# Head sums of two tiles streamed as one: GpSimd scales and adds the squares of two tiles that share a layout of eight heads

## The reference, cut to what matters

```python
x = x + conv(group_norm(x), ...)         # x: 32 images, 384 channels, 1024 pixels; 32 groups

w   = einsum('bnc,oc->bno', xt, qkv_w)   # heads: 12 of d = 32 channels
s   = sum_d((w / ||w||_over_n) ** 2)     # per head and pixel
Pi  = softmax(s * temp, over the 12 heads)
Pi_n = Pi / (sum_n Pi + 1e-8)
dots = einsum('bhn,bhnd->bhd', Pi_n, w * w)
out  = -(w * Pi) / (1 + dots)
y    = einsum('bnc,oc->bno', out, out_w) + out_b
```

## Time and profile before

| | |
|---|---|
| median of 3 runs | 867.25 us (867.11 to 867.55) |
| span of the profiled execution | 864.9 us, first to last instruction |
| PE busy | 851.6 us (98%) |
| DVE busy | 750.2 us (87%) |
| ACT busy | 528.3 us (61%) |
| POOL busy | 232.6 us (27%) |

### The profile page before, as it was taken

The page is one execution under the profiler, slowest core; times in us unless marked ns, Lnnn a source line. Parts: engine busy times, 40 slices in busy tenths (PEclk is TensorE's granted clock), DMA queues, the critical chain, the costliest instruction groups (busy, mean ns, idle before and its releaser), DMA issues.

```text
span 864.9 us, 14022 instructions
## 1 busy us (share of the span) xinstructions
PE 851.6 (98%) x4290; PEld 677.7 (78%) x4290; DVE 750.2 (87%) x1396; ACT 528.3 (61%) x680; POOL 232.6 (27%) x106
## 2 busy tenths in 40 slices
PE   7999999999999999999999999999999999999997
PEld 6767788777787777787777787777887777887776
DVE  7989889898888888888888898888898888898777
ACT  3567656567555677556676556676565675566642
POOL 2432123332123331133331233321233321233300
PEclk9999999999999999999999999999999999999999
DMA  7324665544664544664535654445655446645225
GB/s 279 119 79 153 225 229 185 185 148 169 225 227 161 197 146 181 226 223 160 180 150 198 228 213 168 163 145 220 227 186 196 141 163 225 228 175 186 88 86 197
DMA packets 45259, 157.42 MB, mean 182 GB/s; under 512 B 19866, under 2 KB 23962, under 8 KB 37274
## 3 DMA queue, kind: packets, MB, share of 16 engines
q1 hardware_dynamic: 36856, 154.10, 48.5%
q10 hardware_dynamic: 8354, 2.85, 1.3%
HBM read 104.47 MB, written 52.45 MB: 181 GB/s over the span
## 4 chain that ended last, share of the span: by engine, by line
PE 92%; DVE 4%; issue 1%; DMA 1%; ACT 1%; DVEq 0%; ACTq 0%
PE acc L678 86%; PE spread_ps L800 5%; DVE stats L906 1%; DVE WS L1041 1%; DMA PIB<-pi 0%; DMA X<-in_x 0%; DVE WV L1101 0%; DVE X L1149 0%; PE acc L655 0%; DVE WS L1080 0%; ACT WS L501 0%; DMA pi<-PIT 0%; DVE X L1116 0%; ACT WV L512 0%; PE spread_ps L815 0%
## 5 line engine op out<-in xcount | busy, mean ns | idle before, releaser
L424 POOL TENSOR_TENSOR XL<-XN,XH 128x1024 fp32r<-128x1024 f32 x93 | 222.9, 2414 | 571.7 <-ACT XH L529 548.2
L501 ACT ACTIVATE WS<-acc 128x1024 f32<-128x1024 f32 x96 | 98.4, 1026 | 240.5 <-PE acc L678 197.1
L678 PE MATMUL acc<-XH,W1H 128*128 128x512 f32 x574 | 177.3, 390 | 0.1
L678 PE MATMUL acc<-XH,W1L 128*128 128x512 f32 x574 | 176.8, 389 | 0.0
L678 PE MATMUL acc<-UH,W2H 128*128 128x512 f32 x558 | 172.6, 390 | 1.3 <-ACT WV L512 1.2
L678 PE MATMUL acc<-UH,W2L 128*128 128x512 f32 x558 | 172.3, 390 | 0.0
L678 PE MATMUL acc<-XL,W1H 128*128 128x512 f32 x576 | 146.2, 389 | 0.0
L678 PE MATMUL acc<-UL,W2H 128*128 128x512 f32 x558 | 145.3, 396 | 0.0
L1149 DVE SCALAR_TENSOR_TENSOR X<-acc,bias,X 128x1024 f32<-128x1024 f32 x93 | 116.3, 1276 | 31.0 <-PE acc L678 31.0
L678 PEld LDWEIGHTS acc<-UL,W2H 128*128 128x128 f32 x558 | 102.3, 188 | 32.2 <-issue 11.9
L678 PEld LDWEIGHTS acc<-XL,W1H 128*128 128x128 f32 x576 | 108.0, 188 | 22.7 <-POOL XL L434 0.3
(11 more groups left out here) (119 smaller groups left out, 501.3 us busy)
## 6 DMA issues: line engine op xcount, KB each, us to landing
PIB<-pi SPq DMA_DIRECT2D x94, 528.0 KB, 5.1
X<-in_x SPq DMA_DIRECT2D x31, 1536.0 KB, 6.3
out_y<-X SPq DMA_DIRECT2D x30, 1536.0 KB, 6.5
gathered<-stats_rows ACTq DMA_DIRECT2D x28, 72.0 KB, 5.1
pi<-PIT SPq DMA_DIRECT2D x94, 16.5 KB
X<-in_x SPq DMA_DIRECT2D x3, 512.0 KB, 4.7
out_y<-X SPq DMA_DIRECT2D x1, 1024.0 KB, 6.0
out_y<-X SPq DMA_DIRECT2D x2, 512.0 KB, 2.6
```

Source lines behind the costliest of these rows:

```text
L424: pool.tensor_tensor(XL[:, t, :], XN[:, t, :], XH[:, t, :].bitcast(F32), ALU.subtract).then_inc(xl_done, 1)
L501: act.activation(square_tile(i, t), acc[:, t, :], ACT.Square, accum_out=sumsq[:, t:t + 1]).then_inc(squared, 1)
L678: last = pe.matmul(out[:, h * BANK:(h + 1) * BANK], w[:, k, m * P:(m + 1) * P], r[:, k, h * BANK:(h + 1) * BANK], start=(n == 0 and k == 0 ...
```

## The change

Tiles 0 and 1 get one common layout: eight heads of sixteen channels in each tile, where each had four heads of thirty-two. The weights' columns are ordered so in the prologue (GpSimd's copy of the second weights becomes two copies, and TensorE's turns write other columns); tile 2 keeps its four heads. Since a partition then means the same head in tiles 0 and 1, the scaled squares of both can be added before the head sum. For images 2 to 31:

- GpSimd multiplies the squares of tile 0 and of tile 1 by the inverse sums (one scalar a partition) and adds the two (`pair_squares`: two `tensor_scalar`, one `tensor_tensor`, 128x1024 each), ahead of its `x_lo`.
- TensorE's head sums stream the paired tile and tile 2, eight matmuls where there were twelve.
- VectorE makes the inverse sums of tiles 0 and 1 in `pair_weights`, two small instructions between the last `weigh` and the first `u_lo`; `head_sum_weights` is left with tile 2.
- The rows are spread for two bands (eight heads, four heads) in two transfers of 528 KB where there were three; the first waits for two of the three writes. `attention` takes its sums in two reductions where there was one. The first and last image move all three tiles' rows.

```diff
-HEADSUM_STEPS = 3
+HEADSUM_STEPS = 5
+PAIR_STEPS = 4
+PAIRED = 2
+BAND = (0, 0, 1)
...
+        paired = sb("paired", [P, 2, N])
...
+        def paired_sums(j):
+            return j.follows(PAIRED)
...
-                    for t in tiles:
-                        sp.wait_ge(pi_written[t], rows_moved(j, t, 16))
-                        heads = pi_dram[t * HPT:(t + 1) * HPT].unsqueeze(0)\
-                            .to_broadcast([D, HPT, BLOCKS * QUADS * (QUAD + 1)])
-                        sp.dma_start(PIB[:, t].rearrange("p b n -> p (b n)"), heads).then_inc(pi_spread[t], 16)
+                    for band, of_band in enumerate(BAND_HEADS):
+                        for t in range(of_band.start // HPT, of_band.stop // HPT):
+                            sp.wait_ge(pi_written[t], j.counts(16, 16))
+                        heads = pi_dram[of_band.start:of_band.stop].unsqueeze(0)\
+                            .to_broadcast([P // len(of_band), len(of_band), BLOCKS * QUADS * (QUAD + 1)])
+                        sp.dma_start(PIB[:, band].rearrange("p b n -> p (b n)"), heads).then_inc(pi_spread[band], 16)
...
+            def pair_squares(i):
+                if has(i):
+                    pool.wait_ge(headsum_step, i.counts(HEADSUM_STEPS, 2))
+                    pool.wait_ge(squared, i.counts(T, 2))
+                    pool.wait_ge(scores_done, i.counts(1))
+                    pool.sem_inc(pair_step, 1)
+                    for t in range(2):
+                        pool.tensor_scalar(paired[:, t, :], square_tile(i, t), inv[:, 1, t:t + 1], None, ALU.mult)\
+                            .then_inc(pair_step, 1)
+                    pool.wait_ge(pair_step, i.counts(PAIR_STEPS, 3 - PAIR_STEPS * PAIRED))
+                    pool.tensor_tensor(paired[:, 0, :], paired[:, 0, :], paired[:, 1, :], ALU.add).then_inc(pair_step, 1)
             def step(i):
+                if paired_sums(i):
+                    pair_squares(i)
                 for t in range(T):
                     x_lo(i + 1, t)
...
-                for t in range(T):
+                if paired_sums(i):
+                    pe.wait_ge(pair_step, i.counts(PAIR_STEPS, PAIR_STEPS - PAIR_STEPS * PAIRED))
+                    streams = [(head_temp[:, 0, :], paired[:, 0, :]), (headsum[:, T - 1, :], square_tile(i, T - 1))]
+                else:
+                    streams = [(headsum[:, t, :], square_tile(i, t)) for t in range(T)]
+                for n, (weights, squares) in enumerate(streams):
                     for q in range(QUADS):
...
+            def pair_weights(j):
+                link = chain(headsum_step, j.counts(HEADSUM_STEPS))
+                dve.wait_ge(squared, j.counts(T, 2))
+                dve.wait_ge(scores_done, j.counts(1))
+                link(dve.tensor_scalar(inv[:, 0, 0:2], sumsq[:, 0:2], NORM_FLOOR ** 2, None, ALU.max))
+                link(dve.reciprocal(inv[:, 1, 0:2], inv[:, 0, 0:2]), follows=False)
...
-                    done = dve.tensor_reduce(total, PIB[:, :, :, QUAD], AX_X, ALU.add)
+                    dve.tensor_reduce(total[:, 0:2], PIB[:, 0, :, QUAD].unsqueeze(1).to_broadcast([P, 2, BLOCKS * QUADS]),
+                                      AX_X, ALU.add).then_inc(u_step, 1)
+                    done = dve.tensor_reduce(total[:, 2:3], PIB[:, 1, :, QUAD], AX_X, ALU.add)
...
                 weigh(i - 1, 2)
+                pair_weights(i)
                 u_lo(i - 1, 0)
                 u_lo(i - 1, 1)
```

More of the change, by code:

```diff
@@ L90, in conv_attention @@
     HPT = P // D
+    PAIR_HEADS = 2 * HPT
+    PAIR_D = P // PAIR_HEADS
+    BAND_HEADS = (range(0, PAIR_HEADS), range(PAIR_HEADS, HEADS))
     HALVES = N // BANK
@@ L208, in conv_attention @@
         pi_written = [sem(f"pi_written_{t}") for t in range(T)]
-        pi_spread = [sem(f"pi_spread_{t}") for t in range(T)]
+        pi_spread = [sem(f"pi_spread_{band}") for band in range(BANDS)]
         u_step = sem("u_step")
@@ L260, in pe_spread, with band_rows @@
             return 2 if j.follows(1) else 1
-        def rows_moved(j, t, more=0):
-            return j.counts(16, more - (16 if t == 0 and True else 0))
+        def band_rows(t):
+            return PIB[:, BAND[t], :, 0:QUAD]
+        def paired_sums(j):
+            return j.follows(PAIRED)
         def tile_steps(j, t, steps):
@@ L415, in _ @@
             pool.wait_ge(w2_loaded, 16)
-            pool.tensor_copy(mixed_w2.rearrange("p (m d h) -> p m d h", d=D, h=HPT),
-                             raw_w2.rearrange("p (m h d) -> p m d h", d=D, h=HPT)).then_inc(w2_mixed, 1)
+            for band in BAND_HEADS:
+                columns, h = slice(band.start * D, band.stop * D), len(band)
+                pool.tensor_copy(
+                    mixed_w2.rearrange("p (t c) -> p t c", t=T)[:, :, columns].rearrange("p t (d h) -> p t d h", h=h),
+                    raw_w2.rearrange("p (t c) -> p t c", t=T)[:, :, columns].rearrange("p t (h d) -> p t d h", h=h))\
+                    .then_inc(w2_mixed, 1)
             def x_lo(j, t):
@@ L796, in head_sums @@
                     pe.wait_ge(sm_step, i.counts(SM_STEPS))
-                for t in range(T):
+                if paired_sums(i):
[4 more added lines that the diff above has]
+                for n, (weights, squares) in enumerate(streams):
                     for q in range(QUADS):
-                        block_q = square_tile(i, t).rearrange("p (b q r) -> p q b r", q=QUADS, r=QUAD)[:, q]
-                        last = pe.matmul(scores[q * QUAD:(q + 1) * QUAD, 0:N // QUADS], headsum[:, t, :],
-                                         block_q, start=(t == 0), stop=(t == T - 1))
+                        block_q = squares.rearrange("p (b q r) -> p q b r", q=QUADS, r=QUAD)[:, q]
+                        last = pe.matmul(scores[q * QUAD:(q + 1) * QUAD, 0:N // QUADS], weights, block_q,
+                                         start=(n == 0), stop=(n == len(streams) - 1))
                 last.then_inc(scores_done, 1)
@@ L987, in head_sum_weights @@
                     return
-                link = chain(headsum_step, j.counts(HEADSUM_STEPS))
+                tiles = slice(T - 1, T) if paired_sums(j) else slice(0, T)
+                done = HEADSUM_STEPS - 3 if paired_sums(j) else 0
+                link = chain(headsum_step, j.counts(HEADSUM_STEPS, done))
                 dve.wait_ge(squared, j.counts(T, T))
-                link(dve.tensor_scalar(inv[:, 0, :], sumsq[:], NORM_FLOOR ** 2, None, ALU.max))
-                link(dve.reciprocal(inv[:, 1, :], inv[:, 0, :]))
+                link(dve.tensor_scalar(inv[:, 0, tiles], sumsq[:, tiles], NORM_FLOOR ** 2, None, ALU.max))
+                link(dve.reciprocal(inv[:, 1, tiles], inv[:, 0, tiles]))
                 if j.follows(1):
@@ L995, in head_sum_weights @@
                     dve.wait_ge(temp_kept, 3)
-                link(dve.tensor_tensor(headsum[:], head_temp[:],
-                                       inv[:, 1, :].unsqueeze(2).to_broadcast([P, T, QUAD]), ALU.mult), follows=False)
+                weights = headsum[:, tiles, :]
+                dve.tensor_tensor(weights, head_temp[:, tiles, :], inv[:, 1, tiles].unsqueeze(2).to_broadcast(weights.shape),
+                                  ALU.mult).then_inc(headsum_step, HEADSUM_STEPS - 2 - done)
+            def pair_weights(j):
+                if not has(j):
+                    return
+                link = chain(headsum_step, j.counts(HEADSUM_STEPS))
[3 more added lines that the diff above has]
+                link(dve.reciprocal(inv[:, 1, 0:2], inv[:, 0, 0:2]), follows=False)
             def softmax_shift(j):
```

51 lines of the change are left out of this document (27 added, 24 removed).

## The result

The changed kernel takes 1084.99 us (median of 4 runs, 1082.34 to 1091.92), the kernel before 867.4 us beside it (867.11 to 867.93): 1.252 times the time, 95% interval 1.248 to 1.256. The forecast was slower, 931 us with a range of 860 to 970, so its sign was right and its size was not: 218 us lost where 64 were forecast. The profiled execution took 1091.92 us, its span is 1090.1.

The account below looks back on a forecast made before the run. TensorE was taken to bound the kernel, its chain never leaving it. A 2.6 us wait less 0.45 saved gives 2.15 us an image, 64 us over 30 images: 867.25 + 64 = 931 us, range 860 to 970.

Parts of the forecast that it names:

- The bound and the saving: TensorE's order sets the time; one tile fewer in a head sum saves 0.45 us an image, 13.5 us in all.
- The wait: TensorE waits ahead of every head sum for GpSimd's addition: 2.6 us an image.
- 0.2 + 2d: TensorE's wait at each head sum when two u_lo, two scalings and the addition run one after the other.
- d: Time of one GpSimd scaling of 1024 columns, not in the trace: taken as 1.2 us, range 0.93 to 1.99.
- The hold: VectorE's two u_lo and GpSimd's pair work exclude each other, holding GpSimd the full 2.40 us; chance 0.65.
- The sum: Wait of 2.6 less saving of 0.45 gives 2.15 us an image, 64 us over 30 images.
- The late rows: Rival: first spread waits for the second write, some 0.6 us later, so time stays near 867; chance 0.05.
- VectorE's 0.54 us of new work: Extra reduction and pair_weights on VectorE, covered by 1.02 us idle before L990; otherwise 0.54 us an image.
- The two rivals without a hold: GpSimd undisturbed by u_lo: quick scaling gives 854 to 857 us (chance 0.16), slow scaling about 867 to 912 (0.14).
- the faster one: Rival of no hold and scaling below 1.23 us: 10 to 13.5 us gained, 857 to 854; chance 0.16.

Follow-up runs that it names:

- The halves: Changed kernel without GpSimd's scalings and addition, first band's rows read back in two 264 KB transfers, the first behind the first write alone: 856.9 us, 0.988.

## Why the prediction was right in sign and wrong in size

**The bound and the saving: right.** TensorE's order set the time, and two rounds of a head sum are worth 0.40 us a period by the run with one tile left out; 0.45 was forecast.

**The wait: right in place and mechanism, too small.** It stands where it was forecast, ahead of every head sum, released by GpSimd's addition. By the prediction's own form, 0.2 + 2d, it was 2.6 us with d = 1.2. Measured it is 5.28 us (20.13 - 14.85) in most images. The step that failed is d: "I take 1.2", with 2.41 as the upper end because two operands cost that much (the copy's 1.99 in the range). A scaling of one operand takes 2.84 us, above the two-operand instruction. With it the form gives 0.2 + 5.68 = 5.88; the hold was 1.9 and not the full 2.40, the addition 2.34 and not 2.41, which leaves 5.3. That one operand can't cost more than two was a guess that no row bore out. The nearest row, the select of 128 columns, was brought down to 1.0 and 1.64 by two choices of a fixed part taken from other forms; by its columns alone, 0.292 x 8 = 2.34 us, it would have been nearer, and still short.

The Trainium skill (GPSIMD Engine Reference, section Engine selection) calls one-input work on GpSimd roughly line rate, which gave an estimate of 0.85 us. This trace disagrees: 2.84 us with a pointer, 2.77 with a constant. The measurement decides.

**The hold: right, though less than whole.** The scalings are held by 1.9 of the 2.1 us in which they meet the two `u_lo`; without one a scaling takes 2.85 us. In every fourth image part of the hold falls on VectorE: there the two `u_lo` take 3.20 us in place of 2.36 and the two scalings 6.72 in place of 7.59.

The Trainium skill (SBUF — State Buffer, section Who interferes with whom) has the two engines exclude each other for a whole instruction. For the two-operand addition the runs agree: beside it the 32-column weights, 0.19 us otherwise, took 1.27 and ended with it. For the scaling they don't: the `u_lo` at 550.37 began inside the second scaling, took 1.88 us where 1.22 is usual, and ended at 552.25, before that scaling's end at 552.91; and the same weights took 0.19 us in the middle of the first.

**The term that is missing: TensorE's clock.** The sum passed a wait on at its own length. The empty matmuls show that it, with what follows from it, cost 64 us more: the head sum behind a wait of 5 us took 1.93 us at a clock of 0.50, the products behind it ran partly below full.

With d as measured the sum is 5.3 - 0.4 = 4.9 us an image, 30 images: 147, and 64 by the empty matmuls, 211 of the 218. Not all of the 64 need be slower matmuls. Every fourth image the loop's jump on VectorE leaves 5 to 6 us with nothing to do; one of them on the chain, and the waits of its kind:

```profile
596.84 0.07 DVEq L344
596.91 5.82 issue
602.73 0.07 DVEq L344
602.85 0.09 DVE X L1202
```

```profile
DVE X L1202 <- issue: 26.8, 6, 5.1
```

Five of these stand on the chain, and at the six head sums behind them TensorE waits 5.9 to 6.9 us in place of 5.2, some 6 us in all. In the run with empty matmuls no such wait is left on VectorE, and its head sums keep their period there: the 6 us lie within the 64. No run removes the jump alone, so its share is argued and not shown. The 7 us beyond 211 aren't traced; the run with empty matmuls lies as far above 867.4 + 147.

**The late rows: the rival was right and underpriced.** It was put at 0.6 us at most and a chance of 0.05. `dot` waits 1.3 us an image with the bands alone and 1.65 with two tiles streamed. In the changed kernel it is invisible, since everything is late by more; with GpSimd out of the way it decides between 877 and 857 us. The halves show it: behind the first write they give 20 us back. The pair's weights are part of the same balance: the prediction covered VectorE's 0.54 us of new work by the 1.02 us of its idle time and named 0.54 an image, 16 us, as the price without that cover. The run without the weights gave back as much (877.26 - 860.81), with the rows late. That the sizes agree is partly chance: 0.12 of the 0.54 is a reduction that this run keeps, and the other 0.42 is 12.6 us in 30 images. With the rows in halves the pair's weights stay in and cost nothing (856.9).

**The two rivals without a hold: excluded.** The scaling that starts beside the `u_lo` takes 4.77 us of the 7.59, against 2.85 without them, and that refutes both; and the faster one needed a scaling below 1.23 us besides.

**What stays open.** Of the 16 us that GpSimd's work costs when TensorE doesn't wait for it, 13 stand in TensorE's waits for the weights (21.4 - 8.4); the rest wasn't traced. Why VectorE's jump takes 5 to 6 us in the changed kernel isn't shown. That ScalarE's scaling loses because of the serial chain is read from its rows: with halves TensorE waits 19.1 us at the head sums, against 1.5 with no pair, and 21.5 us are lost (878.41 - 856.9). That no order of the work keeps the pair and beats 867 us is not shown, two were tried.

## What to carry to other kernels

An instruction that the trace doesn't show has no ceiling from another form: measure it alone before it is put on the path. Even the dearest column among GpSimd's rows, 1.02 us for 384, gives 2.72 us for 1024, short of the 2.84 that it took. Work for an idle engine is priced by the whole serial chain that it is put into (who releases it, what it shares with the engine that releases it, who waits for it), and an engine that is idle in a window of 4.6 us can't take three passes over a tile there. When an engine that set the time for the whole span is made to wait, look at its clock behind the wait as well as at the wait; and when two transfers are merged into one, the merged one starts with the last of its parts.

## What the runs showed of the hardware that was not expected

- On GpSimd, 128x1024 f32 with one operand and a scalar takes 2.84 us (2.77 with a constant), the same product with the scalar as a repeated second operand 1.89, an addition of two tiles 2.34.
- VectorE and GpSimd hold each other by form. Beside GpSimd's addition VectorE's 32-column product had a median of 1.10 us, beside the scalings 0.19 us (0.80 in every fourth image); a `u_lo` beside a scaling lost 0.66 us in one image and up to 0.85, beside the repeated-operand form up to 1.7.
- Behind a wait of 5.2 us TensorE's head sum ran at a granted clock of 0.50; with empty matmuls ahead of the same wait it stayed at full, for 64 us in all. With one scaling, behind waits of 2.6 us, it ran at full.
- In the changed kernel VectorE's jump at the end of its loop left 5.1 to 6.1 us without work on the chain, five times; in the run with empty matmuls VectorE has no such wait.
